# ScalarE, not SyncE, issues the stores of results in the inverse stage, one step behind its evictions

## The chip, the cores and the metric

The kernel runs on one NeuronCore of one Trainium2 chip. The metric is device time in microseconds (us) of one execution. The kernel before takes 3080.52 us, the median of three runs (3080.41 to 3087.89).

## The reference, cut to what matters

The kernel computes a Fourier neural operator of four layers on 32 images of 64x64 pixels and 64 channels, and then an attention and a mixture of experts on its tokens. The change touches only the four layers:

```python
for l in range(LAYERS):                                   # 4
    sc = _spectral_conv(h, w1r[l] + 1j * w1i[l], w2r[l] + 1j * w2i[l])   # rfft2, mix 2*16x16 modes, irfft2
    pw = jnp.einsum('bihw,oi->bohw', h, pw_w[l]) + pw_b[l][None, :, None, None]
    y = sc + pw
    mean = y.mean(axis=(0, 2, 3), keepdims=True)
    var = y.var(axis=(0, 2, 3), keepdims=True)
    y = (y - mean) * jax.lax.rsqrt(var + EPS)
    y = y * gamma[l][None, :, None, None] + beta[l][None, :, None, None]
    h = jax.nn.gelu(y, approximate=False)
```

All data is f32. The mean and the variance run over all images, so `y` of a whole layer is written to memory before the next layer can read it.

## The kernel before, in words

A layer has three stages, one after the other, with all engines meeting between them: a forward stage (the transform of `h` to 32x16 modes, by matrix products), a mixing stage (weights times modes), and the inverse stage, in which the change lies. The inverse stage of layer 0 differs in that it reads the small input image in place of `h`. Its loop runs over 16 pairs of images, four quarters each, so 64 steps of 1024 columns. Every engine runs the same loop `over_steps` (line 199), and the helper `At(t, u, q, lag)` says which step an engine works on at a turn when it is `lag` turns behind. The order on each engine is the order of the code; engines wait for one another by semaphores.

In a turn of the inverse stage (`inv`), for its own lagging step:

- SyncE (`inv_loads`, lines 280 to 308) issues all transfers. At each pair's first quarter it issues four loads of the mixed modes `G_d` (line 291, 128 KB each). Then comes the store of the step eight turns back: it waits until both evictions of that step are done (semaphore `eY`, line 295) and issues `ybuf` to `z_d` (line 296, 512 KB). Then it waits until TensorE is through with the step eight turns back (`pY`, line 299) and issues the load of `z` into the place that this frees (line 304, 512 KB; line 302 with 24 KB in layer 0). There are eight places for `z` and only two buffers `ybuf`.
- TensorE transposes (line 371), does the first inverse product for two steps at once on every second turn (line 460), and for the step six turns back adds the pointwise product (line 472) and the second inverse product (line 477) into two banks of PSUM. Line 472 first waits until the evictions of the step two before are done, since two pairs of banks take turns.
- ScalarE applies the gelu to the `z` that was loaded, four turns back (line 594, not in layer 0), and evicts the two banks of the step six turns back to `ybuf` (line 604, twice). Before the first of the two it waits, by the helper `wait` (line 174), for the store of the step two before, which read the same `ybuf` (semaphores `yst`), and for that step's statistics (`eS`).
- VectorE copies the two transposed results (lines 738 and 743) and takes the statistics of each step from `ybuf` (line 750).

So the ring that matters is: an eviction fills one of two `ybuf`; its store must have landed before the eviction two steps later.

Of the kernel before, what the change touches and what calls it, by code (L numbers as in the profile page):

```python
# [61 lines left out]
def build_fno(nc, small, x6, fc0, fc0T, fc0b, wmix, pwT, pwb, gamma, beta, consts, z_d, X_d, G_d, layers=LAYERS):  # L62
# [8 lines left out]
    with ctx:  # L71
# [3 lines left out]
        def sem(name):  # L75
            return ctx.enter_context(nc.semaphore(name))
# [15 lines left out]
        def part(off, n):  # L92
            return work[:, off:off + n]
# [21 lines left out]
        ybuf = [part(16384, 1024), part(17408, 1024)]  # L115
# [30 lines left out]
        yst = [sem(f"yst{u}") for u in range(2)]  # L146

        z_q = z_d.rearrange("(t u) p (q n) -> t u p q n", u=2, q=4)
# [22 lines left out]
        def wait(eng, s, v):  # L171

            if not isinstance(v, int) or v > 0:
                eng.wait_ge(S[s] if isinstance(s, str) else s, v)
# [33 lines left out]
        def enter(eng, who, n):  # L208

            for o in OTHERS[who].split():  # L210
                eng.wait_ge(S[o + "_phase"], n)
# [12 lines left out]
        def _(sp):  # L224
# [55 lines left out]
            def inv_loads(l, first):  # L280
                enter(sp, "sp", 3 * l + 2)
                if first:
                    sp.wait_ge(S["z_zero"], 1)

                def step(t, u, q):
                    a = At(t, u, q, 0)
                    if q == 0 and a.ok:
                        wait(sp, "pI1", l * 32 + a.pair * 2 - 2)
                        for v in range(2):
                            for h in range(2):  # L290
                                sp.dma_start(Gt[u][v * 64:v * 64 + 64, h * 512:h * 512 + 512], G_s[h, a.t, u, v]).then_inc(gl[u], 16)
                    b = At(t, u, q, 8)
                    if b.ok:

                        sp.wait_ge(S["eY"], l * 128 + b.s * 2 + 2)
                        sp.dma_start(z_q[b.t, b.par, :, b.q], ybuf[b.q % 2]).then_inc(yst[b.q % 2], 16)
                    if not a.ok:
                        return
                    wait(sp, "pY", l * 128 + a.s * 2 - 14)
                    o = slice(q * 1024, q * 1024 + 1024)  # L300
                    if first:
                        sp.dma_start(zbuf[u][0:6, o], x6_q[a.t, u, :, q]).then_inc(zl[u][q], 16)
                    else:
                        sp.dma_start(zbuf[u][:, o], z_q[a.t, u, :, q]).then_inc(zl[u][q], 16)
                over_steps(sp, step)
                for u in range(2):
                    sp.wait_ge(yst[u], (l + 1) * 32 * 16)
                leave(sp, "sp")
# [250 lines left out]
        @block.scalar  # L559
        def _(act):  # L560
            act.wait_ge(S["s_w0"], 36 * 16)
            for b in range(PAIRS):
                act.wait_ge(S["a0_mx"], b + 1)
                if b >= 4:
                    act.wait_ge(x0st[b % 4], 32 * (b // 4))
                nc.scalar.activation(plane(Xs0[b % 4], 0), P[2 * (b % 2)][:, :].rearrange("p (k m) -> p k m", m=CM), ACT.Copy).then_inc(S["a0_re"], 1)
            leave(act, "act")

            def mix(l):
                enter(act, "act", 3 * l + 1)  # L570

                def rotate(c):

                    act.wait_ge(xl[c % 4], (l * 2 + c // 4 + 1) * 16)
                    nc.scalar.activation(mixed(c)[64:128, :, 1], mixed(c)[0:64, :, 0], ACT.Copy).then_inc(S["x_re"], 1)  # L575
                rotate(0)
                rotate(1)
                for s in range(MSTEPS):
                    if s % 4 >= 2 and s < 12:
                        rotate(s // 4 * 2 + s % 4)  # L580
                    act.wait_ge(S["pM"], l * 32 + 2 * s + 2)
                    wait(act, gst[s % 2], l * 256 + 32 * (s // 2) if s >= 2 else 0)
                    nc.scalar.activation(Gs[s % 2][:, 512:1024], P[(2 * s + 1) % 8][:, :], ACT.Copy).then_inc(S["eMa"], 1)
                leave(act, "act")

            def inv(l, first):
                enter(act, "act", 3 * l + 2)

                def step(t, u, q):
                    c = At(t, u, q, 4)  # L590
                    z = zbuf[c.par][:, c.q * 1024:c.q * 1024 + 1024]
                    if c.ok and not first:
                        wait(act, zl[c.par][c.q], l * 128 + c.t * 16 + 16)
                        nc.scalar.activation(z, z, ACT.Gelu, bias=bbi, scale=bsc).then_inc(S["z_gelu_c"], 1)  # L594
                    a = At(t, u, q, 6)
                    if a.ok:
                        y = ybuf[a.q % 2].rearrange("p (j s n) -> p s j n", s=2, n=128)
                        for h in range(2):
                            act.wait_ge(S["pY"], l * 128 + a.s * 2 + h + 1)
                            if h == 0:  # L600

                                wait(act, yst[a.q % 2], stores_waited(l, a))
                                wait(act, "eS", l * 128 + a.s * 2 - 2)
                            nc.scalar.activation(y[:, h], P[4 + 2 * (a.q % 2) + h][:, :].rearrange("p (j n) -> p j n", n=128), ACT.Identity, bias=bias0 if first else pwb_c).then_inc(S["eY"], 1)  # L604
                if first:
                    act.wait_ge(S["eStat"], 1)
                act.wait_ge(S["s_parload"], (l + 1) * 128)
                over_steps(act, step)
                act.wait_ge(S["sVar"], l + 1)
                nc.scalar.activation(std, e2, ACT.Sqrt, bias=eps_c).then_inc(S["sRstd"], 1)  # L610
                leave(act, "act")

            def stores_waited(l, a):

                return l * 32 * 16 + (a.pair * 2 + a.q // 2) * 16 if a.s >= 2 else 0

            def fwd(l):
                enter(act, "act", 3 * l)
                b16, b32, b64, b128 = ((l - 1) * n for n in (16, 32, 64, 128))

                def step(t, u, q):
                    a = At(t, u, q, 0)
                    if a.ok:

                        wait(act, fz[a.s % FR], fz_count(l, a.s))
                        nc.scalar.activation(zq[a.s % FR], zq[a.s % FR], ACT.Gelu, bias=bbi, scale=bsc).then_inc(S["z_gelu"], 1)  # L626
                    a = At(t, u, q, 3)
                    if a.ok and a.q % 2 == 1:
                        h = a.q // 2
                        act.wait_ge(S["pF1"], b64 + a.s + 1)  # L630
                        wait(act, "pT2", b64 + a.pair * 4 - 4)
                        for r in range(2):
                            nc.scalar.activation(Ax[a.par].rearrange("p (b c r h i) -> p r h c b i", c=2, r=2, h=2, i=16)[:, r, h],
                                                 P[2 + r][:, :].rearrange("p (i c b) -> p c b i", i=16, c=2), ACT.Copy).then_inc(S["eF1"], 1)
                    a = At(t, u, q, 12)
                    if a.ok and a.q == 0:

                        act.wait_ge(S["pF2"], b32 + a.pair * 2 + 2)
                        wait(act, "pX", b32 + a.pair * 2)
                        for c in range(2):  # L640
                            nc.scalar.activation(Xy.rearrange("p (k g c b) -> p c k g b", k=8, g=4, c=2)[:, c],
                                                 P[5 + c][:, :].rearrange("p (b g k) -> p k g b", g=4, k=8), ACT.Copy).then_inc(S["eF2"], 1)
                    a = At(t, u, q, 14)
                    if a.ok and a.q == 1:

                        act.wait_ge(S["pX"], b32 + a.pair * 2 + 2)
                        if a.pair >= 2:
                            wait(act, xst[a.par], (l - 1) * 256 + a.t * 32)
                        for j in range(4):
                            last = nc.scalar.activation(spectra(a.par, 1, j), spectra_bank(j), ACT.Copy)  # L650
                        last.then_inc(S["eXa"], 1)
                over_steps(act, step, PAIRS // 2 + 2)
                leave(act, "act")
            mix(0)
            inv(0, True)
            for l in range(1, layers):
                fwd(l)
                mix(l)
                inv(l, False)
# [870 lines left out]
```

## Time and profile before

| | us |
|---|---|
| median of three runs | 3080.52 |
| the profiled execution, whole | 3082.53 |
| its span, first to last instruction | 3080.4 |
| TensorE busy in the span | 2629.7 |
| ScalarE busy in the span | 1567.5 |
| inverse stage of layer 0, first to last eviction | 223.0 to 472.8 |
| inverse stage of layer 2, first to last eviction | 1383.4 to 1633.3 |

The trace gives for each instruction its start and duration; an "idle before" is the time that the engine stood still ahead of an instruction, and what ended it. "Landing" of a transfer is when its semaphore has its full count. A wait of an instruction is part of the idle time, not of its duration. SPq is SyncE's queue, ACTq the sequencer of ScalarE, which waits for semaphores ahead of the engine.

### The profile page before, as it was taken

The page shows a single profiled execution, that of the slowest core. Times are in us where ns is not written, and L with a number is a line of the kernel's source. Part 1 is how long each engine was busy: PE and PEld are TensorE (multiplying, and loading weights), DVE is VectorE, ACT ScalarE, POOL GpSimd, SP SyncE. Part 2 cuts the span into 40 slices and gives each one's busy share as a digit, 9 for nine tenths or more (in the row PEclk, how much of TensorE's full clock was granted, in tenths as well). Part 3 has the DMA queues.
Part 4 walks back from the last instruction along what each step waited for, and adds up shares of the span by engine and source line. Part 5 has one row for each costly group of instructions (what it writes and reads, how often), then busy time and mean ns, then how long its engine had stood idle before and what let it go on. Part 6 is the DMA issues. An engine that isn't in the chain of part 4 may idle for free. (4 is left out here: it accounts for less than half of the span.)

```text
span 3080.4 us, 65084 instructions
## 1 busy us (share of the span) xinstructions
PE 2629.7 (85%) x27131; PEld 1694.6 (55%) x27131; DVE 1577.3 (51%) x2552; ACT 1567.5 (51%) x2659; POOL 191.7 (6%) x237
## 2 busy tenths in 40 slices
PE   7559998978899899669998977899799577882999
PEld 4556665648566566566665657566422156642444
DVE  3136666752466677326666752466500376746443
ACT  1213336742456677225566753355499567851333
POOL 0000000000000000000000000000000222220443
PEclk9779999988899999889999998899899888995999
DMA  7845448966899799669988967799665200001432
GB/s 241 246 127 172 168 164 311 322 192 172 252 294 291 273 328 308 140 187 288 295 283 299 322 203 179 233 291 296 221 225 178 51 1 1 1 1 40 94 88 63
DMA packets 243649, 603.67 MB, mean 196 GB/s; under 512 B 28415, under 2 KB 108991, under 8 KB 241087
## 3 DMA queue, kind: packets, MB, share of 16 engines
q1 hardware_dynamic: 243359, 599.51, 62.7%
q8 instruction: 218, 3.57, 0.5%
q14 instruction: 72, 0.59, 0.1%
HBM read 396.12 MB, written 203.93 MB: 195 GB/s over the span
## 5 line engine op out<-in xcount | busy, mean ns | idle before, releaser
L604 ACT ACTIVATE work<-P,small 128x512 f32<-128x512 f32 x512 | 323.8, 683 | 536.0 <-PE P L477 499.3
L371 PE MATMUL P<-cst,work 128*128 128x128 f32 (+1 forms) x3760 | 547.3, 285 | 48.9 <-ACT work L626 13.7
L371 PEld LDWEIGHTS P<-cst,work 128*128 128x128 f32 (+1 forms) x3760 | 410.4, 143 | 206.6 <-issue 157.6
L426 PE MATMUL P<-W,work 128*64 128x64 f32 x4096 | 283.6, 307 | 129.9 <-ACT work L575 129.5
L472 PE MATMUL P<-work,wbd 128*128 128x512 f32 x768 | 371.5, 606 | 0.0
L477 PEld LDWEIGHTS P<-cst,ATs 64*128 64x128 f32 x4096 | 248.4, 187 | 194.1 <-issue 194.1
L426 PEld LDWEIGHTS P<-W,work 128*64 128x64 f32 x4096 | 282.0, 239 | 132.4 <-issue 98.7
L738 DVE COPY ATs<-P 128x512 f32<-128x512 f32 x256 | 177.0, 692 | 327.5 <-PE P L371 327.5
L750 DVE BATCH_NORM_STATS2 W<-work 128x6 f32<-128x512 f32 x512 | 327.1, 680 | 19.8 <-ACT work L604 19.2
L477 PE MATMUL P<-cst,ATs 64*128 64x128 f32 x4096 | 297.5, 285 | 0.0
L780 DVE COPY work<-P 128x512 f32<-128x512 f32 x384 | 247.1, 684 | 73.0 <-PE P L371 72.9
L594 ACT ACTIVATE work<-work,small 128x1024 f32<-128x1024 f32 x192 | 237.3, 1237 | 34.8 <-DMA work<-z_d 34.8
L626 ACT ACTIVATE work<-work,small 128x1024 f32<-128x1024 f32 x192 | 232.8, 1244 | 1.3 <-DMA work<-z_d 1.2
L743 DVE COPY work<-P 128x512 f32<-128x512 f32 x256 | 175.0, 686 | 110.6 <-PE P L460 110.6
L460 PE MATMUL P<-cst,work 64*64 64x128 f32 x4096 | 151.9, 289 | 55.6 <-DMA work<-G_d 49.6
L472 PEld LDWEIGHTS P<-work,wbd 128*128 128x128 f32 x768 | 131.4, 191 | 107.6 <-issue 107.3
L1463 DVE TENSOR_TENSOR mhid<-MH,ms 128x768 f32<-128x768 f32 (+1 forms) x96 | 90.4, 941 | 144.9 <-ACT ms L1389 116.9
L460 PEld LDWEIGHTS P<-cst,work 64*64 64x64 f32 x4096 | 119.1, 141 | 78.8 <-issue 61.1
L786 DVE COPY work<-P 128x512 f32<-128x512 f32 x192 | 132.7, 691 | 46.3 <-PE P L371 46.3
L719 DVE COPY work<-P 128x512 f32<-128x512 f32 x64 | 44.3, 693 | 212.3 <-PE P L426 130.9
L1134 ACT ACTIVATE aE<-AP,am 96x141 f32<-96x141 f32 x384 | 137.9, 380 | 29.0 <-DVE am L1184 28.4
L1389 ACT ACTIVATE ms<-MH 128x768 f32<-128x768 f32 (+1 forms) x96 | 76.5, 797 | 147.4 <-PE MH L1340 147.4
(166 smaller groups left out, 3031.2 us busy)
## 6 DMA issues: line engine op xcount, KB each, us to landing
work<-z_d SPq DMA_DIRECT2D x384, 512.0 KB, 6.0
z_d<-work SPq DMA_DIRECT2D x256, 512.0 KB, 4.0
W<-in_wmix SPq DMA_DIRECT2D x96, 512.0 KB, 6.8
X_d<-work SPq DMA_DIRECT2D x128, 256.0 KB, 5.0
work<-X_d SPq DMA_DIRECT2D x32, 1024.0 KB, 12.4
G_d<-work SPq DMA_DIRECT2D x128, 256.0 KB, 3.3
work<-G_d SPq DMA_DIRECT2D x256, 128.0 KB, 5.4
hz<-z_d SPq DMA_DIRECT2D x64, 512.0 KB, 4.6
```

The source lines that it names most:

```text
L371: return nc.tensor.matmul(out, in_, ident[0:n, 0:n], start=True, stop=True, is_transpose=True)
L426: last = nc.tensor.matmul(P[n % 8][f * 64:f * 64 + 64, i * 64:i * 64 + 64], xm[:, :, x * 4 + y], W[:, 4 * (c + f) + y, x * 64:x * 64 + 64] ...
L460: last = nc.tensor.matmul(P[v][h * 64:h * 64 + 64, i * 128:i * 128 + 128], Gt[a.par][o, x:x + 64], i1c[o, v * 128:v * 128 + 128], start=Tr ...
L472: nc.tensor.matmul(banks[s][:, :].rearrange("p (j n) -> p j n", n=128), pw[0:rows, :], z[:, s], start=True, stop=False)
L477: last = nc.tensor.matmul(banks[s][:, j * 128:j * 128 + 128], ATs[o, a.q % 2, j * 128:j * 128 + 128], i2c[o, s * 128:s * 128 + 128], start ...
L594: nc.scalar.activation(z, z, ACT.Gelu, bias=bbi, scale=bsc).then_inc(S["z_gelu_c"], 1)
L604: nc.scalar.activation(y[:, h], P[4 + 2 * (a.q % 2) + h][:, :].rearrange("p (j n) -> p j n", n=128), ACT.Identity, bias=bias0 if first els ...
L626: nc.scalar.activation(zq[a.s % FR], zq[a.s % FR], ACT.Gelu, bias=bbi, scale=bsc).then_inc(S["z_gelu"], 1)
L738: nc.vector.tensor_copy(ATs[:, a.q % 2, :], P[2 + a.q % 2][:, :]).then_inc(S["eT3"], 1)
L743: nc.vector.tensor_copy(Ai[a.par].rearrange("p (y k) -> p y k", k=2 * KX)[:, :, v * KX + 8 * b:v * KX + 8 * b + 8], P[v][:, :].rearrange(" ...
L750: nc.vector.bn_stats(so, ybuf[a.q % 2][:, h * 512:h * 512 + 512]).then_inc(S["eS"], 1)
L780: nc.vector.tensor_copy(hTq[a.s % 2][:, h * 512:h * 512 + 512], P[h][:, :]).then_inc(S["eT1"], 1)
```

## The change

The store leaves SyncE's loop and goes to ScalarE's, behind the two evictions of a turn. It is then the store of the step before the one just evicted (lag 7, where the evictions have lag 6), and it waits on `eY` as before.

```diff
@@ inv_loads (SyncE)
-                    b = At(t, u, q, 8)
-                    if b.ok:
-
-                        sp.wait_ge(S["eY"], l * 128 + b.s * 2 + 2)
-                        sp.dma_start(z_q[b.t, b.par, :, b.q], ybuf[b.q % 2]).then_inc(yst[b.q % 2], 16)
                     if not a.ok:
                         return
                     wait(sp, "pY", l * 128 + a.s * 2 - 14)
@@ inv (ScalarE)
                             nc.scalar.activation(y[:, h], P[4 + 2 * (a.q % 2) + h][:, :].rearrange("p (j n) -> p j n", n=128), ACT.Identity, bias=bias0 if first else pwb_c).then_inc(S["eY"], 1)
+                    b = At(t, u, q, 7)
+                    if b.ok:
+
+                        act.wait_ge(S["eY"], l * 128 + b.s * 2 + 2)
+                        act.dma_start(z_q[b.t, b.par, :, b.q], ybuf[b.q % 2]).then_inc(yst[b.q % 2], 16)
```

ScalarE's order in the middle of an inverse stage, before: the gelu of a turn, then its two evictions.

```order
410 L594 ACTIVATE work<-work,small 128x1024
411 L604 ACTIVATE work<-P,small 128x4x128 x2
412 L594 ACTIVATE work<-work,small 128x1024
413 L604 ACTIVATE work<-P,small 128x4x128 x2
414 L594 ACTIVATE work<-work,small 128x1024
```

And the same place now; the five lines taken out above have moved the gelu to line 589, the evictions to 599, and the store stands on line 604.

```order
365 L589 ACTIVATE work<-work,small 128x1024
366 L599 ACTIVATE work<-P,small 128x4x128 x2
367 L604 DMA z_d<-work 128x1024
368 L589 ACTIVATE work<-work,small 128x1024
369 L599 ACTIVATE work<-P,small 128x4x128 x2
370 L604 DMA z_d<-work 128x1024
```

A store now stands between each pair of evictions and the next gelu; it carries the result of the turn before.

SyncE's queue in the middle of an inverse stage, before: a store ahead of every load of `z`.

```order
279 L291 DMA work<-G_d 64x512 x4
280 L296 DMA z_d<-work 128x1024
281 L304 DMA work<-z_d 128x1024
282 L296 DMA z_d<-work 128x1024
283 L304 DMA work<-z_d 128x1024
284 L296 DMA z_d<-work 128x1024
285 L304 DMA work<-z_d 128x1024
```

And now, where line 299 is the load of `z`:

```order
169 L291 DMA work<-G_d 64x512 x4
170 L299 DMA work<-z_d 128x1024 x4
171 L291 DMA work<-G_d 64x512 x4
172 L299 DMA work<-z_d 128x1024 x4
```

Only loads are left in it, in their old order, and each waits for TensorE alone.

## Rows read from the trace of the kernel before

**Rows 1.** The page: busy time of each engine, and slices of the span.

```profile
PE 2629.7 (85%) x27131; PEld 1694.6 (55%) x27131; DVE 1577.3 (51%) x2552; ACT 1567.5 (51%) x2659; POOL 191.7 (6%) x237
...
PE   7559998978899899669998977899799577882999
ACT  1213336742456677225566753355499567851333
PEclk9779999988899999889999998899899888995999
DMA  7845448966899799669988967799665200001432
```

**Rows 2.** Busy time by stage: four inverse stages; columns as their first line has them.

```profile
core 0: us, PE busy (x) PEld busy (x) DVE busy (x) ACT busy (x) POOL busy (x), PEclk, DMA share, GB/s
222.00:475.00 253.00, 250.21 (x2452) 154.53 (x2450) 157.28 (x249) 82.24 (x129) 0.00 (x0) 1.00 0.47 166
800.00:1050.00 250.00, 249.93 (x2439) 154.18 (x2438) 155.51 (x245) 148.05 (x187) 0.00 (x0) 1.00 0.87 278
1382.00:1635.00 253.00, 250.72 (x2453) 154.89 (x2452) 157.30 (x248) 150.62 (x190) 0.00 (x0) 1.00 0.87 276
1962.00:2216.00 254.00, 250.91 (x2453) 154.89 (x2452) 156.92 (x247) 150.08 (x190) 0.00 (x0) 1.00 0.87 275
```

**Rows 3.** The page's groups: form | busy, mean ns | idle before, releaser.

```profile
L604 ACT ACTIVATE work<-P,small 128x512 f32<-128x512 f32 x512 | 323.8, 683 | 536.0 <-PE P L477 499.3
...
L472 PE MATMUL P<-work,wbd 128*128 128x512 f32 x768 | 371.5, 606 | 0.0
...
L477 PE MATMUL P<-cst,ATs 64*128 64x128 f32 x4096 | 297.5, 285 | 0.0
```

**Rows 4.** Timeline of TensorE, 899 to 907: start us, us, line, form xcount.

```profile
899.56 1.10 PE L460 MATMUL P<-cst,work 64*64 64x128 f32 x32
900.59 1.98 PE L472 MATMUL P<-work,wbd 128*128 128x512 f32 x4
902.51 1.16 PE L477 MATMUL P<-cst,ATs 64*128 64x128 f32 x16
903.60 0.66 PE L371 MATMUL P<-cst,work 128*128 128x128 f32 x4
904.09 1.88 PE L472 MATMUL P<-work,wbd 128*128 128x512 f32 x4
905.90 1.16 PE L477 MATMUL P<-cst,ATs 64*128 64x128 f32 x16
```

**Rows 5.** Timeline of ScalarE, the same columns.

```profile
887.65 1.26 ACT L604 ACTIVATE work<-P,small 128x512 f32<-128x512 f32 x2 [2.24 <-PE P L477]
891.29 1.26 ACT L604 ACTIVATE work<-P,small 128x512 f32<-128x512 f32 x2 [1.25 <-PE P L477]
...
899.07 1.26 ACT L604 ACTIVATE work<-P,small 128x512 f32<-128x512 f32 x2 [1.01 <-PE P L477]
900.23 1.24 ACT L594 ACTIVATE work<-work,small 128x1024 f32<-128x1024 f32 x1
903.70 1.26 ACT L604 ACTIVATE work<-P,small 128x512 f32<-128x512 f32 x2 [2.23 <-PE P L477]
904.85 1.24 ACT L594 ACTIVATE work<-work,small 128x1024 f32<-128x1024 f32 x1
907.25 1.26 ACT L604 ACTIVATE work<-P,small 128x512 f32<-128x512 f32 x2 [1.16 <-PE P L477]
```

**Rows 6.** Line 604 in layer 2's inverse stage: duration ns min/median/max, starts.

```profile
L604 ACT ACTIVATE work<-P,small x128: 678/686/687, 1383.4 to 1633.3; 128x512 f32<-128x512 f32 x128
```

**Rows 7.** Timeline of SyncE's queue, 896 to 909.

```profile
896.96 0.32 SPq L296 DMA_DIRECT2D z_d<-work  x1
897.33 1.35 SPq L304 DMA_DIRECT2D work<-z_d  x1
898.72 2.62 SPq L291 DMA_DIRECT2D work<-G_d  x4
901.38 0.58 SPq L296 DMA_DIRECT2D z_d<-work  x1
902.01 0.43 SPq L304 DMA_DIRECT2D work<-z_d  x1
904.99 0.32 SPq L296 DMA_DIRECT2D z_d<-work  x1
905.35 0.43 SPq L304 DMA_DIRECT2D work<-z_d  x1
```

**Rows 8.** Line 296, from issue to landing, in layer 0, layer 1, layer 1's end.

```profile
L296 SPq DMA_DIRECT2D z_d<-work x64: 319/343/1133, 224.3 to 473.5; - x64
DMA to landing us min/median/max: 2.6/2.8/5.4
...
L296 SPq DMA_DIRECT2D z_d<-work x59: 319/320/587, 803.9 to 1036.8; - x59
DMA to landing us min/median/max: 2.6/4.8/8.0
...
L296 SPq DMA_DIRECT2D z_d<-work x5: 319/319/320, 1040.2 to 1053.4; - x5
DMA to landing us min/median/max: 2.6/2.6/2.7
```

**Rows 9.** ScalarE's sequencer, waits of line 174: duration ns, first and last start.

```profile
L174 ACTq EVENT_SEMAPHORE  x1: 3454/3454/3454, 903.7 to 903.7; - x1
...
L174 ACTq EVENT_SEMAPHORE  x2: 2377/2960/3542, 887.7 to 891.4; - x2
...
L174 ACTq EVENT_SEMAPHORE  x62: 38/565/1995, 227.6 to 469.3; - x62
```

**Rows 10.** Windows of a mixing and of a forward stage.

```profile
630.00:775.00 145.00, 111.63 (x1670) 96.75 (x1668) 50.25 (x85) 50.22 (x77) 0.00 (x0) 0.88 0.64 166
1643.00:1780.00 137.00, 134.34 (x2104) 90.28 (x2104) 100.01 (x182) 102.31 (x157) 0.00 (x0) 0.97 0.97 336
```

**Rows 11.** Timeline of SyncE's queue at the second inverse stage's end.

```profile
1050.38 3.33 SPq L296 DMA_DIRECT2D z_d<-work  x2
1056.14 3.16 SPq L312 DMA_DIRECT2D work<-z_d  x6
```

## The prediction

> **What bounds the kernel now.** I read the page's slices first, to find the inverse stages: four stretches in which TensorE shows 9 at a granted clock near full speed [rows 1]. The windows over them come next. In each, TensorE is busy for 250 of some 253 us at a clock of 1.00 (2.4 GHz), and in the three stages that load `z` the DMA engines are busy for 0.87 of the time and move some 276 GB/s, in layer 0 for 0.47 [rows 2]. Then I asked who waits: the groups show no idle time ahead of lines 472 and 477, while the evictions stand idle for 536.0 us in all, nearly all of it for TensorE [rows 3]. So TensorE is the bound of this stage, and ScalarE, SyncE and the DMA engines have room, each of them a little. The reader is to see that there is nothing to win in these stages: TensorE has no idle time there that a better order of transfers could remove.
>
> The step is the unit of the sum. In layer 2 the first of 128 evictions starts at 1383.4 and the last at 1633.3 [rows 6]; less 0.6 between the two of a step, that is 249.3 us over 63 intervals, 3.96 us a step. Single steps take turns, since line 460 is done at every second: evictions start at 899.07, 903.70 and 907.25 [rows 5].
>
> **The change part by part.** SyncE loses a store a step. It waited there for ScalarE and had time; its load of `z` now leaves when TensorE is through, together with the start of the evictions, not behind them. Nobody waits for that load in mid-stage, so this gains 0, and line 472 has no idle time that could show a gain [rows 3].
>
> ScalarE gains 64 issues a stage. On SyncE one takes 0.32 us [rows 7, 8]. It stands ahead of the gelu, while the two evictions, 1.26 us together, are still running, and 1.0 to 2.2 us of the engine's idle time come later in the step [rows 5]. Cost by itself: 0.
>
> What costs is the moved store's time. Before, it left right behind its own evictions: those of 903.70 end at 904.96, the store goes at 904.99 [rows 5, 7]. The eviction that needs the buffer again comes two steps after the first, so nearly 8 − 1.3 = 6.6 us remain, against a landing of 4.8 us in the median (8.0 at most) [rows 8]. Now the store of step k is issued in the turn of step k+1's evictions, and the very next evictions, of k+2, need its buffer. A whole step of the room is gone. From the start A of one turn's evictions to the start of the next, ScalarE now needs
>
> x (start of evictions to issue) + L (issue to landing) + about 0.05,
>
> and if that sum is over 3.96 us, each eviction hangs on a store that was itself issued behind the last one: the excess repeats in every step.
>
> x: the sequencer runs ahead of the engine. Its wait for the next turn's buffer begins at 903.7, with the first eviction of 903.70, though another eviction and a gelu stand between them in the order; 3.454 us later it ends, and the next eviction starts at 907.25 [rows 5, 9]. The store will stand ahead of this wait, so x is between 0.05 and, if it has to wait for both evictions to finish, 1.3 us. I take 0.1, as the sequencer's waits do.
>
> L is not shown by any row in its new surroundings. The lower end is 2.6, a store with no load about (the last lines of [rows 8]), and 2.8 in layer 0. The upper end is 4.8, the median beside loads; its maximum of 8.0 belongs to stores issued right behind four loads of `G_d` and will not stand in every step. Between them: the load of `z` starts at the same moment, and the stage's 278 GB/s at a share of 0.87 [rows 2] make some 320 GB/s at most, so 512 KB are 1.6 us of all engines. 2.6 + 1.6 = 4.2. The `G_d` loads, 512 KB in four steps, add 0.4 a step if they are in the way: 4.6. I take 4.5.
>
> A step then takes 0.1 + 4.5 + 0.05 = 4.65 us, 0.69 more than 3.96. Not all of it shows: an eviction may be late by the room that TensorE leaves it. The evictions of 899.07 end at 900.33, and the matmul that needs their banks, the second line 472 from there, starts at 904.09 [rows 4, 5], so 3.7 us are absorbed once a stage. Of 64 steps some 58 run beside loads; at the end there are none and L is 2.6 again. Layers 1 to 3: 58 x 0.69 − 3.7 = 36.3 us each, 109 in all. Layer 0: 0.1 + 2.8 + 0.05 = 2.95, below 3.96; its worst landing of 5.4 makes one eviction some 1 to 2 us late, within the 3.7. Cost 0.
>
> The end of the stage costs nothing more: the last store leaves behind the last evictions in both kernels, and the next stage's loads start when it has landed (at 1056.14 [rows 11]).
>
> Sum against the profiled execution: 3082.5 + 109 = 3191.5. The median of the runs lies 2.0 lower, so 3189.
>
> TensorE's clock: it will be busy for 3.96/4.65 = 85% of the stage. A mixing stage at 77% shows a clock of 0.88, a forward stage at 98% one of 0.97 [rows 10], so something near 0.92 may come. It costs nothing as long as ScalarE's chain is longer than a step of TensorE, 3.96/0.92 = 4.3.
>
> Beside this stands the rule of the Trainium skill (DMA: Bandwidth & Descriptors, "Queues, rings and completion order") that each DMA engine takes turns, packet by packet, between the queues that have work. No row shows two busy queues. By that rule the store would have half of the engines at once and never stand behind `G_d`, L = 4.2, and the sum would be 58 x 0.39 − 3.7 = 19 us a stage, 3137. The same page ("Issuing engines are not separate DMA queues") says that a second issuing engine brings no bandwidth, which speaks against a gain.
>
> **The rivals.**
>
> A, no loss: the stores land in 3.8 us or less on the average. For it speaks 2.6 us alone, and that a step which gets longer thins the traffic. Against it speaks the median of 4.8 where the load was issued about 3 us ahead of the store (902.01 and 904.99 [rows 7]), not at the same time. The deciding point is L = 3.81; below it the 3.7 us of room take up all single late stores, and the time is 3080. This is the case that ends on the other side, not slower. The same 3080 comes out if the sequencer passes the evictions before they may start and issues the store right after `eY` of its own step, since that is when SyncE issues it now. The rows speak against it: the sequencer's next wait begins only as an eviction starts, 903.7 with 903.70, 891.4 with 891.29, 887.7 with 887.65 [rows 5, 9]. The Trainium skill (Advanced Engine Details and Errata, "Sequencer Loop") would allow it: engine instructions wait in a queue of their own while others are read. The trace disagrees in these three places, and I give this way 0.02 of A's chance.
>
> B, the issue waits for the running evictions: x = 1.3. The load of `z` is then 1.3 us ahead, and L falls to perhaps 3.4 (4.5 less most of this). A step takes 4.75, 0.79 more: 42 a stage; layer 0 with 1.3 + 2.8 + 0.05 = 4.15 loses 60 x 0.19 − 3.7 = 8. Sum 134: 3214. With L at 4.5 as well, a step is 5.85, and 58 x 1.89 − 3.7 = 106 a stage and layer 0's 8 make 3406.
>
> C, L stays at the 4.8 of the rows: a step of 4.95, 58 x 0.99 − 3.7 = 54 a stage, 3241.
>
> D, a gain: SyncE's loads leave earlier, above all those of `G_d`, for which TensorE waits at the start of a stage. But there no store stands ahead of them, so it would be 2 us at most: 3078.
>
> **How the numbers follow.** The forecast with L from 4.0 to 4.7 has 0.52, C 0.16, B 0.16 (three quarters of it below 3290), A 0.12, D 0.04. The likeliest gives 3189. The range leaves out A, D and the high end of B, 0.20 together: 3100 (L = 4.0: a step of 4.15, 58 x 0.19 − 3.7 = 7 a stage, 3102) to 3290 (C with room for some of B). Under 0.3% (9 us) a measurement of this kernel can't be told from no change; A falls within, with 0.01 from the forecast's low end: slower 0.83, same 0.13, faster 0.04.
>
> **What would show it.** In the changed kernel the evictions' idle time ends on the landing of `z_d`'s store, not on TensorE; lines 472 stand idle for ScalarE; the start-to-start time of evictions is even, about 4.65 us in layers 1 to 3, and the turns of short and long steps are gone; layer 0's stage is as long as before; the DMA share of the other three falls to about 0.75. The store's issue stands 0.1 us behind the first eviction's start, for B 1.3. I am wrong if TensorE still has no idle time there (A), or if layer 0 is longer too (B).

## The result: 138 us slower

The changed kernel takes 3220.4 us (median of four runs, 3208.8 to 3226.6), the kernel before 3082.0 beside it; the ratio is 1.0441, 95% interval 1.0408 to 1.0474. The forecast was 3189, in a range of 3100 to 3290. The profiled execution takes 3226.6 us, 144 more than that of before.

The page of the changed kernel, with the lines that answer to [rows 1, 3]:

```profile
PE 2677.7 (83%) x27131; PEld 1711.8 (53%) x27131; DVE 1572.0 (49%) x2552; ACT 1568.0 (49%) x2659; POOL 191.8 (6%) x237
...
q1 hardware_dynamic: 206495, 465.28, 48.9%
q10 hardware_dynamic: 36864, 134.23, 10.6%
...
L599 ACT ACTIVATE work<-P,small 128x512 f32<-128x512 f32 x512 | 323.8, 683 | 682.3 <-PE P L472 352.3
...
L467 PE MATMUL P<-work,wbd 128*128 128x512 f32 x768 | 397.9, 643 | 102.4 <-ACT work L599 102.0
```

The stores' 134 MB are a queue of their own now (q10). The matmuls that reuse the banks (line 467, 472 before) had no idle time and have 102 us, for the evictions; TensorE's busy time is 48 us longer, and the two together, some 150, are the loss. The evictions of layers 0, 1, 2 and 3 begin and end at:

```profile
L599 ACT ACTIVATE work<-P,small x128: 678/686/687, 220.4 to 470.2; 128x512 f32<-128x512 f32 x128
...
L599 ACT ACTIVATE work<-P,small x128: 677/685/689, 800.0 to 1095.2; 128x512 f32<-128x512 f32 x128
...
L599 ACT ACTIVATE work<-P,small x128: 676/684/688, 1427.3 to 1730.8; 128x512 f32<-128x512 f32 x128
...
L599 ACT ACTIVATE work<-P,small x128: 678/685/687, 2059.6 to 2357.7; 128x512 f32<-128x512 f32 x128
```

Layer 0 is as long as before, 249.8 us. Layer 1 takes 295.2, layer 2 303.5, layer 3 298.1, against the 249.9 of [rows 6]; together some 147 more, which accounts for the whole difference. The windows that answer to [rows 2]:

```profile
220.00:470.00 250.00, 249.59 (x2442) 153.91 (x2438) 155.91 (x246) 80.06 (x127) 0.00 (x0) 1.00 0.46 164
800.00:1080.00 280.00, 249.82 (x2332) 150.39 (x2334) 146.62 (x234) 140.12 (x177) 0.00 (x0) 0.96 0.74 238
```

Where the loads of `z` run, TensorE is down to 0.89 of the window, the DMA engines' share to 0.74 (0.87 before). How one step hangs on the next is seen in ScalarE's timeline, to be read with [rows 5]:

```profile
907.61 0.69 ACT L599 ACTIVATE work<-P,small 128x512 f32<-128x512 f32 x1 [1.24 <-issue]
907.66 0.33 ACTq L604 DMA_DIRECT2D z_d<-work  x1
908.20 0.68 ACT L599 ACTIVATE work<-P,small 128x512 f32<-128x512 f32 x1
908.76 1.24 ACT L589 ACTIVATE work<-work,small 128x1024 f32<-128x1024 f32 x1
912.56 0.69 ACT L599 ACTIVATE work<-P,small 128x512 f32<-128x512 f32 x1 [2.56 <-issue]
912.62 0.33 ACTq L604 DMA_DIRECT2D z_d<-work  x1
```

and in TensorE's:

```profile
908.56 1.16 PE L472 MATMUL P<-cst,ATs 64*128 64x128 f32 x16
909.65 0.66 PE L366 MATMUL P<-cst,work 128*128 128x128 f32 x4
```

The store leaves 0.05 us behind the start of the first eviction. The next eviction's product was there at 909.7, yet it starts at 912.56, when the store of 907.66 had landed (4.83 us later, at 912.49). The view calls this idle time "issue" and names no DMA. That it is the wait for the store is seen in the row of ScalarE's sequencer, whose wait on line 174 lasts 4.46 us from 908.1, up to the landing:

```profile
L174 ACTq EVENT_SEMAPHORE  x1: 4456/4456/4456, 908.1 to 908.1; - x1
```

It is so nearly everywhere: of the 62 evictions of a layer that reuse a buffer, 58, 57 and 59 in layers 1 to 3 start 0.07 us behind the landing of its store; in the kernel before it was 13 to 16, without a loss. In layer 1 the idle time called "issue" makes 118.4 us, the waits for TensorE 36.9:

```profile
ACT work L599 <- issue: 118.4, 49, 5.9
ACT work L599 <- PE P L472: 36.9, 15, 9.1
```

### The profile page after: what moved, and what is told of

The parts are those of the page before. It is cut to its first block and busy times, and to the rows that moved or that the text cites. A ratio compares the mean times of both kernels' runs of the same rounds, so it can differ in the third digit from the quotient of the medians.

```text
span 3224.4 us, 65084 instructions
## 1 busy us (share of the span) xinstructions
PE 2677.7 (83%) x27131; PEld 1711.8 (53%) x27131; DVE 1572.0 (49%) x2552; ACT 1568.0 (49%) x2659; POOL 191.8 (6%) x237
## 5 line engine op out<-in xcount | busy, mean ns | idle before, releaser
L467 PE MATMUL P<-work,wbd 128*128 128x512 f32 x768 | 397.9, 643 | 102.4 <-ACT work L599 102.0
L472 PEld LDWEIGHTS P<-cst,ATs 64*128 64x128 f32 x4096 | 256.0, 192 | 206.1 <-issue 138.7
L472 PE MATMUL P<-cst,ATs 64*128 64x128 f32 x4096 | 305.4, 290 | 0.0
L780 DVE COPY work<-P 128x512 f32<-128x512 f32 x384 | 247.1, 684 | 72.0 <-PE P L366 72.0
L743 DVE COPY work<-P 128x512 f32<-128x512 f32 x256 | 174.3, 683 | 84.8 <-PE P L455 84.7
L786 DVE COPY work<-P 128x512 f32<-128x512 f32 x192 | 132.7, 691 | 46.8 <-PE P L366 46.8
L930 PE MATMUL HP<-hz,hf 64*128 64x512 f32 x512 | 134.3, 637 | 15.8 <-ACT hz L898 15.3
```

The costliest lines, as they stand in the source:

```text
L467: nc.tensor.matmul(banks[s][:, :].rearrange("p (j n) -> p j n", n=128), pw[0:rows, :], z[:, s], start=True, stop=False)
L472: last = nc.tensor.matmul(banks[s][:, j * 128:j * 128 + 128], ATs[o, a.q % 2, j * 128:j * 128 + 128], i2c[o, s * 128:s * 128 + 128], start ...
L743: nc.vector.tensor_copy(Ai[a.par].rearrange("p (y k) -> p y k", k=2 * KX)[:, :, v * KX + 8 * b:v * KX + 8 * b + 8], P[v][:, :].rearrange(" ...
L780: nc.vector.tensor_copy(hTq[a.s % 2][:, h * 512:h * 512 + 512], P[h][:, :]).then_inc(S["eT1"], 1)
```

## The experiments

Each was run in turns with the kernel before on the same chip, and its ratio is against those runs, whose medians are 3085.9 (e1 to e4), 3087.1 (e5 to e8) and 3086.3 us (e9, e10). "Stage" is the time from the first to the last pair of evictions of layer 1; "landing" the mean from issue to landing of the stores of its steps 2 to 56, worked out from the trace's issues and semaphores.

| | median us | ratio, 95% interval | stage | landing |
|---|---|---|---|---|
| before | 3082.0 | 1 | 249.5 | 5.1 |
| changed | 3220.4 | 1.0441 (1.0408 to 1.0474) | 294.7 | 4.6 |
| e1, four buffers | 3084.1 | 0.9992 (0.9983 to 1.0001) | 249.3 | 6.4 |
| e2, same turn | 3084.0 | 0.9996 (0.9987 to 1.0005) | 249.3 | 5.7 |
| e3, SyncE late | 3127.2 | 1.0130 (1.0115 to 1.0146) | 266.7 | 4.9 |
| e4, no loads of `z` | 3084.8 | 0.9997 (0.9987 to 1.0007) | 249.4 | 3.3 |
| e5, small loads of `G_d` | 3106.3 | 1.0083 (1.0051 to 1.0115) | 268.2 | 4.2 |
| e6, load after the landing | 3437.1 | 1.1128 (1.1112 to 1.1145) | 370.5 | 6.0 |
| e7, SyncE tied to evictions | 3268.3 | 1.0584 (1.0568 to 1.0601) | 306.7 | 4.1 |
| e8, four buffers, three late | 3209.4 | 1.0383 (1.0346 to 1.0420) | 284.9 | 4.3 |
| e9, load behind the evictions | 3126.6 | 1.0126 (1.0110 to 1.0141) | 262.7 | 4.1 |
| e10, load behind the gelu | 3177.9 | 1.0284 (1.0263 to 1.0304) | 283.7 | 4.5 |

The theory is R, the ring of two buffers; the first rival is Q, the second queue as such.

**e1, four buffers.**

```diff
-        ybuf = [part(16384, 1024), part(17408, 1024)]
+        ybuf = [part(16384, 1024), part(17408, 1024), part(12288, 1024), part(13312, 1024)]
-        yst = [sem(f"yst{u}") for u in range(2)]
+        yst = [sem(f"yst{u}") for u in range(4)]
```

(and `% 2` taken out where they are used, with the counts waited for).

> The changed kernel with four buffers ybuf in place of two (12288 to 14335 of the work area is free in the inverse stage); ScalarE still issues each store one step late, with the next evictions. Theory R (the ring of two buffers: the evictions of k+2 hang on the store of k, which leaves only with the evictions of k+1, so a step is 0.05 + landing + about 0.1 us): the landing has three steps, nearly 12 us, so the step is TensorE's 3.96 us again, the time 3082 us within 6, and line 472's matmuls wait for no eviction. Rival Q (the loss comes from the second queue itself: stores on ScalarE's queue land late, or the issue holds up ScalarE's sequencer): 3200 to 3225 stays.

The loss is gone, 3084.1, though the stores land later than in any other kernel here. A landing of 6.4 us in the median costs nothing when the buffer is needed only three steps later:

```profile
DMA to landing us min/median/max: 4.0/6.4/8.1
```

Q falls here: queue, issue and delay are those of the changed kernel.

**e2, same turn.**

```diff
-                    b = At(t, u, q, 7)
+                    b = At(t, u, q, 6)
```

> The changed kernel, but ScalarE issues the store in the turn of its own evictions (lag 6, not 7). Its sequencer then stands still for the 1.3 us until both evictions have finished, and the gelu starts some 0.5 us later; the two buffers stay. Theory R: the landing has a step more, some 6.6 us as before, so 3082 to 3095 us. Rival Q: 3200 or more, since the queue is the same and the sequencer is held up longer.

3084.0: two buffers, the same queue, and the loss is gone as well. ScalarE's timeline shows the price, a sequencer that waits for its own evictions and a gelu 0.4 us later, which idle time of the engine takes up:

```profile
903.42 1.26 ACT L599 ACTIVATE work<-P,small 128x512 f32<-128x512 f32 x2 [2.31 <-DMA z_d<-work]
904.71 0.33 ACTq L604 DMA_DIRECT2D z_d<-work  x1
905.09 1.24 ACT L589 ACTIVATE work<-work,small 128x1024 f32<-128x1024 f32 x1 [0.40 <-ACT work L599]
```

**e3, SyncE late.** On the kernel before, ahead of the store:

```diff
                         sp.wait_ge(S["eY"], l * 128 + b.s * 2 + 2)
+                        if b.s < 63:
+                            sp.wait_ge(S["pY"], l * 128 + b.s * 2 + 3)
```

> The kernel before, stores on SyncE's queue, but SyncE also waits for the first product of the next step (pY) before it issues a store: the store leaves as late as in the changed kernel, in the old queue, ahead of the load. Theory R: slower, too; with the landing of 4.8 us that the kernel before shows a step is about 5.0 us, 3235 us; with the shorter 4.4 us of less traffic 3180, so 3180 to 3250. Rival Q: 3082, since nothing was put on another queue.

Slower in the old queue too, as R says, so the late issue is enough; but by 41 us against the runs beside it, where I had expected 100 to 170. Its landings of 4.9 us should have made steps of 5.0, and they are 4.3. The reason I formed: the store waited for TensorE's product of the next step, not for the evictions of it. A late eviction didn't make the next store late, and the excess could not repeat. e7 tests this.

**e4, no loads of `z`.**

```diff
-                    if first:
+                    if first or a.pair >= 2:
                         sp.dma_start(zbuf[u][0:6, o], x6_q[a.t, u, :, q]).then_inc(zl[u][q], 16)
```

(and the gelu of those pairs takes a scale of zero). This kernel and e5 leave data out of the result; they are there for the time alone.

> The changed kernel; in layers 1 to 3 the loads of z from the third pair on are replaced by the small loads of layer 0 (24 KB of the image), so their data is left out of the result, and the gelu there takes a scale of zero. Everything else is the same, the queues too. Theory R: stores land in about 2.9 us as in layer 0, 0.05 + 2.9 + 0.1 is below 3.96, so 3082 us within 8 and a DMA share near 0.5. Rival Q by a sequencer that is held up: 3200 or more, whatever the traffic.

3084.8: with landings of 3.3 us the late store costs nothing, as in layer 0.

```profile
DMA to landing us min/median/max: 2.6/3.1/4.8
```

Two conditions must meet: the store has one step of room, and traffic makes its landing longer than a step.

**e5, small loads of `G_d`.**

```diff
+                        n = 512 if l == 0 or a.pair < 2 else 8
-                                sp.dma_start(Gt[u][v * 64:v * 64 + 64, h * 512:h * 512 + 512], G_s[h, a.t, u, v])
+                                sp.dma_start(Gt[u][v * 64:v * 64 + 64, h * 512:h * 512 + n], G_s[h, a.t, u, v][:, 0:n])
```

> The changed kernel; in layers 1 to 3 the loads of G_d from the third pair on move 8 columns instead of 512, so most of that data is left out of the result. It prices the part of the landing that these loads cause. Theory R with G_d in the way (my term of 0.4 us a step): landings fall from 4.7 to about 4.3 us, 3150 us, 3125 to 3180. Rival (turns between the queues keep G_d out of the store's way): 3205 or more.

3106.3, lower than expected. Landings fell to 4.2 us in layer 1 and 3.9 in layers 2 and 3, whose stages took 250.7 and 251.4 us. That is the point from which the loss sets in: 3.9 and the 0.12 around it are TensorE's own 4.0 us. Near it little decides: 4.2 in layer 1 cost 19 us, 3.9 in the others 1 to 2. So without the bytes of `G_d` some 110 to 120 of the 138 us are gone, but they cost only on top of `z` (e4 loads `G_d` in full and loses nothing).

**e6, load after the landing.**

```diff
                     wait(sp, "pY", l * 128 + a.s * 2 - 14)
+                    if not first and a.s >= 9:
+                        sp.wait_ge(yst[(a.s - 9) % 2], l * 32 * 16 + ((a.s - 9) // 2 + 1) * 16)
```

> The changed kernel, but SyncE issues the load of z only when the store that left with the evictions of the freed step has landed; all transfers stay. Theory R with a landing that is long because load and store move together: the store lands in 2.7 to 3.4 us, a step is TensorE's again, 3085 to 3110 us. Rival (landings are long because memory or the DMA engines are busy in all, whatever the order): 3180 or more.

The greatest miss, 3437. I had overlooked that the landing which releases the load also releases the next eviction, and that the next store leaves 0.05 us behind it. So load and store left together at every step:

```profile
878.93 0.33 SPq L301 DMA_DIRECT2D work<-z_d  x1
...
878.94 0.69 ACT L601 ACTIVATE work<-P,small 128x512 f32<-128x512 f32 x1 [3.92 <-PE P L474]
878.99 0.33 ACTq L606 DMA_DIRECT2D z_d<-work  x1
...
DMA to landing us min/median/max: 5.6/6.1/6.8
```

The steps are 6.2 us in the mean, 0.2 over the mean landing. The miss measures what I had to estimate: a store that leaves with a load in the other queue lands in 6.0 us, not in the 4.2 of my sum.

**e7, SyncE tied to evictions.** On the kernel before:

```diff
-                        sp.wait_ge(S["eY"], l * 128 + b.s * 2 + 2)
+                        sp.wait_ge(S["eY"], l * 128 + b.s * 2 + (3 if b.s < 63 else 2))
```

> The kernel before, stores on SyncE's queue, but each store also waits for the first eviction of the next step (eY), where e3 made it wait for TensorE's product. Theory R, sharpened: the loss repeats in each step since a late eviction makes the next store late; in e3 a late eviction didn't, so it lost 45 us only. Tied to evictions, a step is 0.7 + landing + 0.1, with landings of 4.1 to 4.8 us 4.9 to 5.6: 3230 to 3350 us. Rival (SyncE's queue is simply the better one, stores stand ahead of the loads in it): about as e3, 3125 to 3165.

3268.3, slower than the changed kernel, without any DMA of ScalarE. The store leaves 0.71 us behind the start of the first eviction, and 0.71 + 4.1 + 0.1 is 4.9 where steps of 5.0 are measured. So what makes the loss large is that each late eviction delays the next store; e3, without that tie, lost a quarter of this kernel's 181 us, though its stores landed later. Here they land in 3.6 us in the median, the shortest beside full loads:

```profile
DMA to landing us min/median/max: 3.1/3.6/7.6
```

Each stands ahead of its load in one queue, but so it does in the kernel before and in e3, where the means are 5.1 and 4.9 against 4.1 here; the steps are longer here and the traffic thinner (235 GB/s, and 293 before). No run separates the two.

**e8, four buffers, three late.** On e1:

```diff
-                    b = At(t, u, q, 7)
+                    b = At(t, u, q, 9)
```

(and one more round of ScalarE's loop, so that the last stores leave).

> The kernel with four buffers of e1, but ScalarE issues each store three steps late (lag 9), so that again the next evictions need its buffer. Theory R: what counts is the time from a store's issue to the eviction that reuses its buffer, one step as in the changed kernel; 3200 to 3240 us. Rival (two buffers are too few for transfers in flight, four are enough): 3082 as e1.

3209.4. The loss is back with four buffers. The count of buffers is nothing by itself; what counts is how many steps lie between the issue of a store and the eviction that reuses its buffer.

**e9 and e10, the load's place in the step.** In each, one wait of SyncE is added ahead of the load:

```diff
+                    if a.s >= 8:
+                        sp.wait_ge(S["eY"], l * 128 + a.s * 2 - 14)
```

```diff
+                    if not first and a.s >= 8:
+                        sp.wait_ge(S["z_gelu_c"], (l - 1) * 64 + a.s - 4)
```

> The changed kernel, but SyncE issues the load of z only when both evictions of the freed step are done, as it did in the kernel before; so the store (0.05 us behind the first eviction's start) has 1.2 to 1.3 us of a lead over the load in each step. Theory P (the landing hangs on where the load starts against the store: together 6.0 us as in e6, apart less): landings of 3.5 to 4.3 us, 3085 to 3150 us. Rival V (the mean landing is set by the traffic of a step, not by its phase): 4.6 us and more, 3200 or above.

> As e9, but in layers 1 to 3 the load waits for the gelu that follows those evictions, so it leaves some 2.4 us behind the first eviction's start and the store. Theory P: nearly the landing of a store alone in the three steps of four without G_d, 2.7 to 3.4 us, 3082 to 3110 us. Rival V: 3200 or above.

Both beat the changed kernel with the same transfers, so the mean landing is not set by traffic alone, and V falls. e9 came as expected:

```profile
DMA to landing us min/median/max: 2.7/3.8/7.4
```

e10 did not: 3177.9, landings of 4.5 us and not 3.

```profile
DMA to landing us min/median/max: 2.6/4.4/7.1
```

A load that leaves 2.4 us behind the store takes 5.0 us to land in mid-stage, and the next store leaves while it still runs (that is so in e9 as well, where the load takes 5.3); the landings of the stores that meet `G_d` are 5.5 to 5.9 us in the mean of a layer. P holds for the direction, and of the three places tried (together with the store in e6, 1.3 and 2.4 us behind it) 1.3 is the best, but why 2.4 is worse isn't shown, and I have no formula for the landing.

## Why the prediction was right

**The mechanism.** TensorE was the bound with nothing to gain; the store lost a step of its room; each eviction then hung on a store issued with the last one. e1, e2 and e8 show that the room is the cause, e4 that it needs the loads, e7 and e3 that the tie to the evictions repeats it, and nearly every eviction of layers 1 to 3 starts on a landing. Layer 0 cost nothing, as forecast.

**x.** Taken as 0.1 from the place of the sequencer's wait [rows 9]; measured 0.05, in layer 0 too. Rival B, an issue that waits for the running evictions at 1.3 us, is out. So is the thought that the sequencer passes the turn's two evictions while they still wait: no store left earlier than 0.05 us behind the start of the first. Layer 0, where the eviction waits for TensorE and not for its buffer, has the plainest case: the sequencer's wait on line 174 is over at 263.34, the eviction starts at 265.06, and the store, whose own eviction was long done, leaves only at 265.11.

**L, the mis-sized term.** Taken as 4.5; the means of layers 1 to 3 are 4.6, 4.8 and 4.7, near the 4.8 of rival C. My working was wrong in both directions, and that the errors nearly cancelled was luck. Together with a load a store takes 6.0 (e6) and not 4.2. But in the changed kernel they don't leave together: TensorE gains a lead while ScalarE waits, up to the two pairs of banks, and since the load hangs on TensorE and the store on ScalarE, the load of a step leaves ahead of the store that would go with it by 3.7 to 5.7 us in the median of a layer. Only 8 to 11 of 53 stores leave within 0.5 us of any load; these land in 5.1 to 5.8 us in the mean, the others in 4.6 to 4.7. The 0.4 us for `G_d` were too small as well: without its bytes the landings fell by 0.5 us in layer 1 and by 0.8 to 1.0 in layers 2 and 3 (e5, at shorter steps).

**The step.** 4.65 forecast; 4.8, 5.0 and 4.9 measured from step 3 to step 57: the landing and 0.12 beside it, with some steps in which TensorE is the later one. I compared with 3.96, which counts the short steps at the stage's end; the steps beside loads take 4.01. With 4.90 and 4.01 the same sum, 58 x 0.89 − 3.7, is 48 us a stage and 144 in all: the measured difference of the profiled executions. So the form of the sum holds, and L and the base are its errors. Its 58 steps and its 3.7 us aren't tested apart: the 54 intervals from step 3 to 57 make the same 48 us without a deduction.

**The signs.** The DMA share fell to 0.74 (0.75 forecast), the waits are where they were said to be. The steps are not even: they run from 2.8 to 8.6 us with the landings. The granted clock was 0.96, not 0.92.

**The rule of turns.** The Trainium skill (DMA: Bandwidth & Descriptors, "Queues, rings and completion order") has each DMA engine take turns between queues. What e6 shows agrees in kind: load and store end 0.5 us apart after leaving 0.06 apart, while in one queue (e7) the store lands after 4.1 us in the mean and the load behind it after 6.3. The 3137 us that I worked out by it were too low: I took 4.2 us for a store beside a load, where e6 shows 6.0, and nothing for `G_d`, where e5 shows 0.5 to 1.0.

**Rival A** needed a mean landing under 3.81. The measured border is near 3.9 (e5), and the landings were beyond it. Of D's gain nothing is seen: layer 0 is as long as before, the others longer.

None of these versions beats the kernel before: where the loss is gone the stage takes TensorE's 249 us, and e1's interval holds 1.

## What to carry to other kernels

When a store is moved later in a ring of buffers, count the time from its issue to the write that reuses its buffer, and compare it with the landing under load, not with the landing alone. If the issue itself hangs on that write's predecessor, an excess repeats at every step; if it hangs on something that runs ahead, most of it is absorbed (181 us in e7, 41 in e3). The second queue by itself was harmless here once the ring had a step more: e1 and e2 cost nothing, and gained nothing.

## What the runs showed of the hardware

- A DMA that ScalarE issues doesn't wait for the activation that runs: it goes 0.05 us behind the start of the first of the two ahead of it, and takes 0.33 us of the sequencer (0.32 on SyncE).
- Load and store of 512 KB that leave together in two queues land in 5.7 and 6.0 us (e6), where a store alone takes 2.6.
- At TensorE's full pace and the same 293 or 294 GB/s, the stores land after 5.1 us in the mean in one queue with their loads (before), after 5.7 in a second queue 1.3 us behind a load (e2), after 6.4 in a second queue together with one (e1). So at that pace the second queue made the stores slower, and hid nothing.
- The queue alone doesn't decide this: at steps of 4.3 us and some 273 GB/s the stores of e9 (second queue, the load 1.3 us behind) land after 4.1 us, those of e3 (one queue, the load right behind) after 4.9. When the load leaves against the store matters as well (e6, e9 and e10 differ in that alone).
